# Attention's row maxima: turned by VectorE in squares of 32 instead of by TensorE, split on Pool, with the query stacks stored half by half

## What is computed

```python
# B, L, C = 4, 1024, 256; 16 heads of 16
attn = jnp.einsum('bhqd,bhkd->bhqk', q, k) * scale
attn = jax.nn.softmax(attn, axis=-1)
out = jnp.einsum('bhqk,bhkd->bhqd', attn, v)
```

## Time and profile before

| | |
|---|---|
| median of 3 runs | 1182.5 us (1182.16 to 1183.19) |
| profiled execution, its own time | 1181.48 us |
| its span, first to last instruction | 1179.7 us |
| busy: PE / DVE / ACT / POOL | 92% / 86% / 65% / 30% |
| mean granted TensorE clock | 0.949 |
| `attend`, from the profile's slices | about 101 us to 785 us |

### The profile page before, as it was taken

The page is one execution under the profiler, slowest core; times in us unless marked ns, Lnnn a source line. Parts: engine busy times, 40 slices in busy tenths (PEclk is TensorE's granted clock), DMA queues, the critical chain, the costliest instruction groups (busy, mean ns, idle before and its releaser), DMA issues. The chain is left out here.

```text
span 1179.7 us, 22856 instructions
## 1 busy us (share of the span) xinstructions
PE 1083.5 (92%) x8540; PEld 595.9 (51%) x8540; DVE 1016.5 (86%) x2168; ACT 768.6 (65%) x932; POOL 352.6 (30%) x316
## 2 busy tenths in 40 slices
PE   7899999999999999999999999998984059999998
PEld 6775333333333333333333333347773048888897
DVE  8999889999999999999999999716998985766663
ACT  4551378888888888888887888863565014555653
POOL 2657812202220221122022000022100023765675
PEclk9997699999999999999999999999997559999999
DMA  7787664504422441343044100036532022554443
GB/s 240 252 267 232 148 101 98 96 18 78 75 57 39 81 77 31 65 79 70 22 84 75 21 12 17 17 103 214 178 108 95 0 72 65 152 146 122 111 112 36
DMA packets 84681, 113.95 MB, mean 97 GB/s; under 512 B 25056, under 2 KB 57568, under 8 KB 84576
## 3 DMA queue, kind: packets, MB, share of 16 engines
q1 hardware_dynamic: 66256, 69.82, 20.0%
q0 software_dynamic: 15024, 36.17, 17.2%
q10 hardware_dynamic: 3296, 6.56, 1.5%
HBM read 73.31 MB, written 38.27 MB: 95 GB/s over the span
## 5 line engine op out<-in xcount | busy, mean ns | idle before, releaser
L810 DVE TENSOR_REDUCE b_max_halves<-banks 128x1 f32<-128x512 f32 x1024 | 626.7, 680 | 14.3 <-PE banks L878 14.2
L748 ACT ACTIVATE b_probs<-banks 128x1024 f32<-128x1024 f32 x512 | 520.7, 1027 | 146.4 <-PE banks L929 146.4
L878 PE MATMUL banks<-b_k,b_q 62*128 62x512 f32 x1024 | 398.7, 470 | 6.7 <-DVE b_max_halves L810 1.8
L929 PE MATMUL banks<-b_q,b_k 64*128 64x512 f32 x1024 | 385.8, 456 | 3.8 <-DMA b_q<-b_max_rows 3.5
L900 PE MATMUL banks<-b_probs,b_v 128*17 128x256 f32 (+1 forms) x3840 | 315.5, 401 | 0.2 <-ACT b_probs L748 0.2
L929 PEld LDWEIGHTS banks<-b_q,b_k 64*128 64x128 f32 x1024 | 156.9, 186 | 224.2 <-issue 167.8
L878 PEld LDWEIGHTS banks<-b_k,b_q 62*128 62x128 f32 x1024 | 162.0, 190 | 41.6 <-DVE b_max_halves L810 39.3
L900 PEld LDWEIGHTS banks<-b_probs,b_v 128*17 128x17 f32 x3840 | 63.9, 95 | 165.6 <-issue 95.9
L551 POOL TENSOR_TENSOR b_att<-b_out,b_rec_spread 128x512 f32<-128x512 f32 x32 | 41.1, 1284 | 311.5 <-DMA b_rec_spread<-reciprocals 311.2
L483 POOL DMA_DIRECT2D b_q<-q_stacks x60 | 31.8, 533 | 227.8 <-PE banks L900 215.6
L1849 DVE TENSOR_TENSOR e_hTl<-e_hT,e_hTh 128x512 fp32r<-128x512 f32 x64 | 47.6, 745 | 48.3 <-ACT e_hT L1603 48.3
(11 more groups left out here) (259 smaller groups left out, 1477.9 us busy)
## 6 DMA issues: line engine op xcount, KB each, us to landing
e_w<-in_w SPq DMA_DIRECT2D x16, 1024.0 KB
q_stacks<-a_parts SPq DMA_DIRECT2D x32, 256.0 KB, 4.0
k_stacks<-a_parts SPq DMA_DIRECT2D x32, 256.0 KB, 4.1
b_q<-q_stacks POOLq DMA_DIRECT2D x30, 256.0 KB, 5.3
b_k<-k_stacks POOLq DMA_DIRECT2D x30, 256.0 KB, 6.4
v_tiles<-a_v ACTq DMA_DIRECT2D x8, 544.0 KB, 3.7
b_rec_spread<-reciprocals SPq DMA_DIRECT2D x128, 32.0 KB, 1.8
attended<-b_att SPq DMA_DIRECT2D x128, 32.0 KB, 2.7
```

Source lines behind the costliest of these rows:

```text
L748: nc.scalar.activation(pr[:, S % NP, u], ps[:, 2 * u:2 * u + 2, :], ACT.Exp, scale=D ** -0.5).then_inc(s_ex[u], 1)
L810: v.tensor_reduce(mxp[:, (k // NB) % 2, s, p, t, kh:kh + 1], ps[:, bank(last), :], AX.X, ALU.max)\
L878: nc.tensor.matmul(ps[:, bank(last), :], qs[g][stack, p, at:at + P], ks[g][stack, p, CH * kh:CH * kh + CH], start=True, stop=True).then_in ...
L929: return nc.tensor.matmul(ps[:, 2 * u + s, :], ks[g][stack, u, P * kt:P * kt + P], qs[g][stack, u, CH * h:CH * h + CH], start=True, stop=True)
```

## The change

1. **Turning.** TensorE no longer turns `b_max`. VectorE transposes a tile of 128x32 float32 in squares of 32 by 32, in SBUF (`turn`). After it, row m of the square of query block b is the row of maximum m for 32 queries. `plan`, `free` and the ring items for the turn go away: the ring holds maxima products alone.
2. **Splitting.** Leading and trailing part are made before the turn, on tiles of 128x16 (`parts`), by Pool; for the first two half groups by VectorE. VectorE turns two reduces after the combine, at u = 1 of step `LATE`.
3. **Order of `b_q`.** The free axes become half, pair, query. A group's q is loaded by 8 transfers instead of 4, with pieces of 2 KB instead of 4 KB; so a group takes 13 transfers instead of 9. `project_qkv` loads group 0 in the same way.
4. **The row transfers** are still eight, each now of 16 pieces of 128 bytes instead of 4 of 512 bytes.
5. **Pool's order** in a half group is now `scale`, `parts`, `load`.

```diff
-LD = 9 * 16
+LD = 13 * 16
...
+        for p in range(2):
+            for to, n in ((0, 16), (16, 32)):
+                sp.dma_start(q[HR * s + to:HR * s + to + n, :, p, :].bitcast(F32),
+                             qst[b][G * g + s + 2 * p][0:n, :].rearrange("r (h c) -> r h c", c=CH)).then_inc(s_ld, 16)
...
+        def parts(e, eng, n):
+
+            eng.wait_ge(s_mx, n + 1)
+            e.tensor_copy(mp[:, :, 0, :], mx[:].rearrange("p s q t -> p s (q t)")).then_inc(s_parts, 1)
+            eng.wait_ge(s_parts, 2 * n + 1)
+            e.tensor_tensor(mp[:, :, 1, :], mx[:].rearrange("p s q t -> p s (q t)"), mp[:, :, 0, :].bitcast(F32),
+                            ALU.subtract).then_inc(s_parts, 1)
...
+        def rows(eng, g, h, stacks=(0, 1)):
+            for s in stacks:
+                to = qs[g][HR * s + RS:HR * s + HR, h].bitcast(F32).rearrange("r p (t b c) -> r (p t) b c", b=P // VW, c=VW)
+                for b in range(P // VW):
+                    m = VW * b + 4 * NT * s
+                    eng.dma_start(to[:, :, b, :], mT[m:m + 4 * NT, :]).then_inc(s_row[h], 16)
...
             def body(i, first, last):
                 for hg in range(NH):
                     g = hg // 2
+                    if hg > 1 or not first:
+                        tail.scale(pool, g_, 8 * i + hg - 2, hg % 2, 4 * i + (hg - 2) // 2 + 1)
+                    if not (first and hg == 0) and not (last and hg == NH - 1):
+                        parts(g_, pool, NH * i + hg + 1)
                     if hg % 2 == 0 and not (last and g > 0):
...
-                    if hg > 1 or not first:
-                        tail.scale(pool, g_, 8 * i + hg - 2, hg % 2, 4 * i + (hg - 2) // 2 + 1)
...
-            def rows(n, m, last):
-
-                rows_ = ps[0:4 * NT, bank(last), 0:P]
-                dve.wait_ge(s_mm, m + 1)
-                v.tensor_copy(mT[:, 0, :], rows_).then_inc(s_lead, 1)
-                dve.wait_ge(s_lead, n + 1)
-                v.tensor_tensor(mT[:, 1, :], rows_, mT[:, 0, :].bitcast(F32), ALU.subtract).then_inc(s_ra, 1)
+            def turn(n):
+
+                dve.wait_ge(s_parts, 2 * n + 2)
+                v.transpose(mT[:], mp[:].rearrange("p s r m -> p (s r m)").bitcast(F32)).then_inc(s_ra, 1)
...
                     for kt in range(KT):
+                        for u in range(2):
+                            for k in ahead(i, hg, kt, u):
+                                reduce(k)
+                            if u == 0 and kt == LATE and more:
+                                combine(NH * i + hg + 1)
+                                if first and hg == 0:
+                                    parts(v, dve, 1)
+                            if u == 1 and kt == LATE and more:
+                                turn(NH * i + hg + 1)
...
-            def rows(hg, n, items, m, last):
-                pe.wait_ge(s_mx, hg + 1)
-                free(n, items, m)
-                nc.tensor.matmul(ps[:, bank(last), 0:P], mx[:], ident[:], is_transpose=True, start=True, stop=True)\
-                    .then_inc(s_mm, 1)
```

More of the change, by code:

```diff
@@ L589, in attend @@
         two = lambda n: [sem(f"{n}0"), sem(f"{n}1")]
-        qs = [group0[0]] + [sb(f"b_q{g}", [P, 2, L], F32R) for g in range(1, NG)]
+        qs = [group0[0]] + [sb(f"b_q{g}", [P, 2, 2, CH], F32R) for g in range(1, NG)]
         ks = [group0[1]] + [sb(f"b_k{g}", [P, 2, L], F32R) for g in range(1, NG)]
@@ L597, in attend @@
         mxp = sb("b_max_halves", [P, 2, 2, 2, NT, 2])
-        mx = sb("b_max", [P, P])
-        mT = sb("b_max_rows", [4 * NT, 2, P], F32R)
+        mx = sb("b_max", [P, 2, 2, NT])
+        mp = sb("b_max_parts", [P, 2, 2, 2 * NT], F32R)
+        mT = sb("b_max_rows", [P, VW])
         osb, rb = tail.osb, tail.rb
@@ L629, in bodies, with ahead, bank @@
                 body(i, i == 0, i == B - 1)
[L631 to L663, removed]
+        def ahead(i, hg, kt, u):
+            k = NB * (NH * i + hg) + PER * kt + AHEAD + 2 * u
+            return [k, k + 1] if k < MAXS * B else []
+        def bank(k):
+            return RING + k % NR
+        def parts(e, eng, n):
[4 more added lines that the diff above has]
+                            ALU.subtract).then_inc(s_parts, 1)
         def pair(k):
@@ L700, in body @@
             def body(i, first, last):
-                n = before(i, first)
                 for hg in range(NH):
@@ L711, in body @@
                     if not (last and hg == NH - 1):
-                        sp.wait_ge(s_ra, n["rows"] + hg + 1)
+                        sp.wait_ge(s_ra, NH * i + hg + 2)
                         rows(sp, (hg + 1) // 2 % NG, (hg + 1) % 2)
@@ L804, in _, with reduce, combine @@
             v = nc.vector
-            def reduce(k, m, last):
+            def reduce(k):
                 s, kh, t, p = pair(k)
-                dve.wait_ge(s_mm, m + 1)
-                v.tensor_reduce(mxp[:, (k // NB) % 2, s, p, t, kh:kh + 1], ps[:, bank(last), :], AX.X, ALU.max)\
+                dve.wait_ge(s_mm, k + 1)
+                v.tensor_reduce(mxp[:, (k // NB) % 2, s, p, t, kh:kh + 1], ps[:, bank(k), :], AX.X, ALU.max)\
                     .then_inc(s_mr, 1)
-            def combine(n, h):
+            def combine(n):
@@ L827, in _ @@
-            v.memset(ps[:, PV, :], 0.0)
[L828 to L833, removed]
+                v.tensor_tensor(mx[:], mxp[:, n % 2, :, :, :, 0], mxp[:, n % 2, :, :, :, 1], ALU.max).then_inc(s_mx, 1)
+            def turn(n):
+                dve.wait_ge(s_parts, 2 * n + 2)
+                v.transpose(mT[:], mp[:].rearrange("p s r m -> p (s r m)").bitcast(F32)).then_inc(s_ra, 1)
@@ L834, in _ @@
+            v.memset(ps[:, PV, :], 0.0)
+            for k in range(AHEAD):
+                reduce(k)
                 if k == NB - 1:
-                    dve.wait_ge(s_zero, 1)
-                    combine(0, 0)
+                    combine(0)
+                    parts(v, dve, 0)
+                    turn(0)
             def body(i, first, last):
-                at, items = plan(last)
-                n = before(i, first)
                 for hg in range(NH):
+                    more = not (last and hg == NH - 1)
@@ L842, in body @@
                     for kt in range(KT):
[L843 to L851, removed]
+                        for u in range(2):
+                            for k in ahead(i, hg, kt, u):
+                                reduce(k)
+                            if u == 0 and kt == LATE and more:
[4 more added lines that the diff above has]
+                                turn(NH * i + hg + 1)
+                            if u == 1 and kt == KT - 1 and not (first and hg == 0):
@@ L856, in _, with maxima @@
         def _(pe):
[L857 to L870, removed]
+            def maxima(k):
                 g = k // (2 * NB) % NG
@@ L906, in _ @@
             pe.wait_ge(s_ld[0], LD)
[L907 to L912, removed]
+            for k in range(AHEAD):
+                maxima(k)
             pe.wait_ge(s_one[0], 32)
             def body(i, first, last):
[L916 to L924, removed]
                 def scores(g, h, S, u, s):
@@ L950, in body @@
                             scores(g, h, S, u, 0)
-                            for x in range(2):
-                                ring(hg, kt, u, x)
+                            for k in ahead(i, hg, kt, u):
+                                maxima(k)
                             scores(g, h, S, u, 1).then_inc(s_st[u], 1)
```

34 lines of the change are left out of this document (10 added, 24 removed).

## The result

The kernel after takes 1271.6 us (median of 4 runs, 1263.7 to 1273.3) against 1182.9: a ratio of 1.074, 95% interval 1.0715 to 1.0761. The forecast was slower, but 1227; the range ended at 1257.

The account below looks back on a forecast made before the run. PE was taken to bound `attend`, leading DVE by a hair. 1181.5 - 14 (turn) + 58 (12 loads meeting row transfers) + 1 (first half group) = 1226.5, or 1227 against the median; range 1190 to 1257.

Parts of the forecast that it names:

- What bounds the kernel, and the turn: In `attend` PE leads DVE by a hair; turning on VectorE saves 0.45 us in each of 30 half groups, -14 us.
- Pool's order decides: Pool's load, now behind `parts`, is in the queues beside SP's row transfers in 12 half groups: +58 us, bounds +30 to +78.
- The eighth starts at +5.9 and lands at +10.9 (4.95 us) to +11.9 (6.0): Eighth row transfer beside a load, in us from the combine, against a deadline of +8.04: stall 2.8 to 3.9 us.
- the term of 12 x 4.8 = +58 us: Cost of 12 half groups whose load meets the row transfers, 4.8 us each for stall and what follows.
- Rival (b): Rows wait until the whole load is through: 8.5 us at each of 12 meetings, +102, 1271 us; chance 8%.
- What follows a wait: After each PE stall for rows beside a load, another 1.5 us is lost beyond the wait itself.
- The estimate by a packet's turn: DMA engines change queues only after a whole packet: rows beside a load delayed 2.6 to 4.8 us, sum +45 to +70.
- The first half group: `load(0, 2)` has four more issues before the rows; the existing stall grows by 0 to 2 us: +1 us.
- The four more issues in the loop, "hold nobody up": Pool's four more issues per load, 0.53 us each, delay nothing: the tiles are wanted four half groups later.
- (a): Rows slip through beside the load in the 12 half groups, meetings cost nothing: faster, 1169 us; chance 13%.
- (c): Pool is late with the split, delaying the turn and DVE's reduces: +15 on top of the forecast, 1242 us; chance 12%.
- (d): The turn's gain and a mild meeting of load and rows cancel, within 0.2%; chance 4%.

Follow-up runs that it names:

- experiment 6: Kernel before (TensorE's turn) with the new layout; Pool loads, waits for the combine, then scales; SP sends rows before the store: 1185.5 us, ratio 1.0023.
- 4: Kernel after with Pool's order load, parts, scale (load at its old moment) and SP's order rows, store: 1175.1 us, ratio 0.9911.
- experiments 1: Kernel before with only Pool's load moved: Pool scales, waits for the combine, then loads beside the row transfers: 1269.9 us, ratio 1.073.
- 8: Kernel after with only Pool's order changed, to load, scale, parts: 1184.0 us, ratio 1.0016.
- experiment 2: Kernel before with the new query stack layout alone (13 transfers per load), TensorE's turn kept: 1198.0 us, ratio 1.0133.

## Why the prediction was right in its course and wrong in its size

*What bounds the kernel, and the turn.* Right. The transpose takes 0.20 us (0.19 taken), the cast and subtraction on Pool 0.20 and 0.22, done 0.6 us before the turn. A half group without a load went from 20.3 to 19.8 us, and experiment 6 against 4 gives that to the turn with its split. The half group at each border of batches lost its extra 0.6 us besides, in every version with the new turn; by the code that was `free`, whose first items of a batch waited for all reduces before them, but no run isolates it.

*Pool's order decides.* Right, shown by experiments 1 and 8: put into the kernel before, the late load costs 87 us; with the order undone the kernel after is back at 1184. The 12 meetings, their place and the wait for DMA of `b_max_rows` came as forecast.

*"The eighth starts at +5.9 and lands at +10.9 (4.95 us) to +11.9 (6.0)"*: this step failed. It starts at 387.60 + 7/8 x 5.32 = 392.3, +6.2, and PE goes on at 399.94, +13.9: 7.7 us. So the term of 12 x 4.8 = +58 us was too small: the stall is 5.6 us on average instead of 2.8 to 3.9, and a meeting costs 7.8 us (27.6 - 19.8), in all +94 (88 against the old period of 20.3). These 36 us are the greater part of the 46 by which the profiled execution (1272.7) lies over the sum of 1226.5; 11 more lie outside the loop, where the sum had nothing, and the turn gave 2 us more than taken.

I took the delay that other transfers had beside a load as a property of the meeting, while it depends on what is queued already. At the eighth row transfer 11 of the load's 13 transfers had been issued, and the DMA engines stayed full for 7 us more. In the earlier trace rows only some 2 us of traffic was left after the eighth (152 to 154), and for the load that is "younger here" I added only 0.5 us. The median of the earlier trace rows hid the same rule: the first of those four sums landed after 4.4 us, the last after 6.8, like the load's own transfers issued beside it. From 427.5 to 428.2, and from 430.1 to 430.6:

```profile
b_sums<-b_out SPq DMA_DIRECT2D x1, 2.0 KB, 4.4
```
```profile
b_q<-q_stacks POOLq DMA_DIRECT2D x1, 256.0 KB, 6.6
b_k<-k_stacks POOLq DMA_DIRECT2D x1, 256.0 KB, 7.5
b_sums<-b_out SPq DMA_DIRECT2D x1, 2.0 KB, 6.8
```

These sums landed by about 437, before the load's traffic ended (438.7). So it is the traffic queued before a transfer, not the whole load, that fits all of these; for the eighth row transfer the two are nearly the same. Rival (b), "the rows wait until the whole load is through", with 8%, was close to that: its price of 8.5 us per meeting compares with 7.8 measured. That its sum, 1271, meets the measured time is in part luck: its meetings come to 102 us instead of 94, and it has nothing for the 11 us outside the loop.

*What follows a wait*: 1.5 us taken. Measured: 7.8 less the wait, 5.6 on average in the 12 half groups, so 2.2; in the one shown the clock was 0.50 from 399 to 405.

*The estimate by a packet's turn.* By the rule of the Trainium skill (DMA: Bandwidth & Descriptors, "Queues, rings and completion order") that a DMA engine drains a whole packet before it changes queues, the prediction's estimate was 2.6 to 4.8 us of delay. Measured are 7.7 less 1.7, that is 6.0 us. In the first half group of before, SP's queue moved no packet for over 6 us.

The same section of the Trainium skill (DMA: Bandwidth & Descriptors, "Queues, rings and completion order") also says that a transfer's semaphore write lands only after every earlier write of that DMA engine, across its queues. That would delay the signal. In the first half group of before not the signal alone was late: all 64 packets of the row transfers moved when the load's traffic was all but through. Whether in the kernel after the last data or the signal comes last, no run here separates.

*The first half group*: 1 us taken, 2.4 measured (27.6 - 24.5, less 0.7 in the period before).

*The four more issues in the loop, "hold nobody up"*: right for the kernel after, where the scale comes first. It would have been wrong with the old order: experiment 2 lost 15 us in the median. In its profile eleven meetings of scale and combine make 0.6 us each, and the one late store makes 5.

*Rivals (a), (c), (d)* did not come: PE waited at least 3.6 us in each of the 12 half groups, and DVE waited for Pool's split only once, 0.6 us.

## What to carry to other kernels

In this kernel a small transfer that is waited for was as late as the bulk traffic queued before it. So before moving a bulk load, write down when its traffic ends and which deadlines lie before that. If a transfer's latency beside a load is read from a trace, read it for each transfer, and together with how much of the load had been issued before it and was still to come. And look at operations like the combine: a short VectorE operation with two SBUF inputs waited here for a long Pool operation, so a change that only shifts Pool by 2 us can lengthen the path.

## What the runs showed of the hardware that was not expected

Eight transfers of 2 KB on SP's queue landed 13.8 to 13.9 us after the combine beside a load of 1.85 MB on Pool's queue, with 32 pieces in all or with 128, and with a wait of only 0.6 us beside 0.8 MB. In the kernel before, 2 KB sums issued 0.7 and about 3 us after a load's first issue took 4.4 and 6.8 us to land, against 2.0 beside no load. A VectorE `tensor_tensor` of 128x16 took 0.73 to 0.74 us in the rows shown instead of 0.17 when Pool's of 128x512 had begun before it, and ended within 0.05 us of it.
